# Two transformer layers on one core: every rectified feed-forward bank leaves PSUM through ScalarE's copy

## The reference

```
h = jnp.concatenate([x, -x], axis=-1)
h = s0 * _conn_dense(k0, h)
h = jax.nn.relu(h) * 2          # 512 features: four banks of 128 a sequence ("ff0")
h = s1 * _conn_dense(k1, h)
h = jax.nn.relu(h) * 2          # again four banks a sequence ("ff1")
h = s2 * _conn_dense(k2, h)
```

## Time and profile before

| | |
|---|---|
| median of 3 runs | 815.64 us (815.59 to 815.67) |
| the profiled execution | 815.69 us, its span 813.9 us |
| granted TensorE clock | 0.995 of full speed on the mean |
| TensorE matmul busy | 749.1 us, 92% of the span |
| ScalarE busy | 755.6 us, 93% |
| VectorE busy | 554.7 us, 68% |
| GpSimd busy | 64.1 us, 8% |
| chain that ended last | PE 55%, ACT 25%, DVE 10%, issue 7%, DMA 2% |

### The profile page before, as it was taken

The page is one execution under the profiler, slowest core; times in us unless marked ns, Lnnn a source line. Parts: engine busy times, 40 slices in busy tenths (PEclk is TensorE's granted clock), DMA queues, the critical chain, the costliest instruction groups (busy, mean ns, idle before and its releaser), DMA issues.

```text
span 813.9 us, 18430 instructions
## 1 busy us (share of the span) xinstructions
PE 749.1 (92%) x6975; PEld 250.4 (31%) x6975; DVE 554.7 (68%) x1185; ACT 755.6 (93%) x847; POOL 64.1 (8%) x84
## 2 busy tenths in 40 slices
PE   8888889999999999999999999999998889999997
PEld 5122222342323223232332323232332223333332
DVE  7788786778784687757876677856877476377322
ACT  4899989999999999999999999999989899899986
POOL 4111110000020100201011010101001000000000
PEclk9899999999999999999999999999999999999999
DMA  3916435502256025440265212660353403302500
GB/s 110 196 31 157 97 99 145 128 2 78 79 121 155 14 79 136 107 110 14 92 152 135 53 53 85 144 163 1 106 130 90 120 1 128 82 1 88 133 14 14
DMA packets 46000, 74.12 MB, mean 91 GB/s; under 512 B 7360, under 2 KB 23360, under 8 KB 45776
## 3 DMA queue, kind: packets, MB, share of 16 engines
q1 hardware_dynamic: 44096, 67.31, 32.3%
q0 software_dynamic: 1744, 5.44, 2.2%
q10 hardware_dynamic: 64, 0.10, 0.0%
HBM read 36.84 MB, written 35.65 MB: 89 GB/s over the span
## 4 chain that ended last, share of the span: by engine, by line
PE 55%; ACT 25%; DVE 10%; issue 7%; DMA 2%; SPq 1%; DVEq 0%; ACTq 0%
ACT probs L858 24%; PE ps_pv L1044 23%; PE ps_s L1025 12%; PE ps_misc L883 8%; PE ps_misc L879 6%; PE ps_misc L884 5%; PE ps_misc L872 1%; SPq L576 1%; DMA k_c<-parts_dram 1%; DVE pv_sb L1607 1%; ACT ff_out L810 1%; DVE h_lo L1283 0%; DVE h_hi L1281 0%; DMA k_ab<-thirds_dram 0%; DVE tmp L1145 0%
## 5 line engine op out<-in xcount | busy, mean ns | idle before, releaser
L858 ACT ACTIVATE probs<-ps_s 128x1024 f32<-128x1024 f32 x768 | 723.0, 1062 | 27.8 <-PE ps_s L1025 26.2
L1044 PE MATMUL ps_pv<-probs,v_aug 128*32 128x512 f32 x3072 | 410.2, 606 | 6.3 <-DVE pv_sb L1607 5.6
L1025 PE MATMUL ps_s<-q_ab,k_ab 32*128 32x512 bf16 x896 | 88.4, 384 | 24.4 <-ACT probs L858 21.9
L1025 PE MATMUL ps_s<-q_c,k_c 32*128 32x512 f32 (+1 forms) x640 | 81.8, 500 | 16.6 <-ACT probs L858 16.1
L1044 PEld LDWEIGHTS ps_pv<-probs,v_aug 128*32 128x32 f32 x3072 | 61.2, 108 | 98.0 <-issue 81.6
L883 PE MATMUL ps_misc<-h_hi,k_w 128*128 128x512 f32 x192 | 87.9, 458 | 3.4 <-DVEq L1285 1.2
L884 PE MATMUL ps_misc<-h_lo,k_w 128*128 128x512 f32 x192 | 75.7, 394 | 0.0
L1607 DVE STREAM_TRANSPOSE pv_sb<-ps_pv 128x512 f32<-128x512 f32 x48 | 34.4, 717 | 56.8 <-PE ps_pv L1044 53.0
L883 PEld LDWEIGHTS ps_misc<-h_hi,k_w 128*128 128x128 f32 x192 | 35.8, 187 | 105.5 <-issue 56.2
L1025 PEld LDWEIGHTS ps_s<-q_ab,k_ab 32*128 32x128 bf16 x896 | 22.6, 91 | 144.5 <-ACT probs L858 117.3
L1025 PEld LDWEIGHTS ps_s<-q_c,k_c 32*128 32x128 f32 (+1 forms) x640 | 30.9, 182 | 109.4 <-ACT probs L858 89.5
(11 more groups left out here) (168 smaller groups left out, 619.9 us busy)
## 6 DMA issues: line engine op xcount, KB each, us to landing
parts_dram<-qk_parts SPq DMA_DIRECT2D x38, 256.0 KB, 3.0
parts_dram<-qk_parts SPq DMA_DIRECT2D x16, 512.0 KB, 2.8
q_c<-parts_dram SPq DMA_DIRECT2D x32, 256.0 KB, 5.0
k_c<-parts_dram SPq DMA_DIRECT2D x32, 256.0 KB, 7.1
thirds_dram<-qk_thirds SPq DMA_DIRECT2D x42, 192.0 KB, 2.7
q_ab<-thirds_dram SPq DMA_DIRECT2D x56, 128.0 KB, 3.2
k_ab<-thirds_dram SPq DMA_DIRECT2D x56, 128.0 KB, 3.6
thirds_dram<-qk_thirds SPq DMA_DIRECT2D x28, 128.0 KB, 2.7
```

Source lines behind the costliest of these rows:

```text
L858: nc.scalar.activation(probs[:, U.slot(s), 2 * half:2 * half + 2], ps_s[:, 2 * pair:2 * pair + 2], ACT.Exp, bias=-SCALE[U.layer] * BOUND[U ...
L1025: ins = nc.tensor.matmul(ps_s[:, bank, :], k[row:row + n, slot, c * P:(c + 1) * P], q[row:row + n, slot, :], start=True, stop=True)
L1044: ins = nc.tensor.matmul(ps_pv[32 * j:32 * j + 32, :], v_aug[:, U.v, c, a:a + 32], probs[:, U.slot(s), j, :], start=c == 0 and not odd, st ...
```

## The change

The table `DIRECT` becomes empty. All that asks it (`taker`, `split_ff`, the plan of who frees which bank) then treats the nine banks as the other 55: Relu on ScalarE into `ff_out`, copy and subtraction on VectorE from there.

```
-DIRECT = (("ff0", 1, 0), ("ff0", 2, 0), ("ff0", 3, 0), ("ff0", 4, 0), ("ff0", 5, 0), ("ff0", 6, 1), ("ff1_b", 6, 3), ("ff1_b", 7, 1), ("ff1_b", 7, 3))
+DIRECT = ()
```

## The result

The changed kernel takes 818.36 us (median of 8 runs, 817.5 to 819.59), the kernel before 815.62 (8 runs, 814.66 to 817.06). The ratio is 1.0033, 95% interval 1.0022 to 1.0043: 2.7 us slower, where 3.4 was forecast. The profiled execution took 819.59 us with a span of 817.8, which is 1.2 us above the median, so its total isn't compared; its stretches are. One run of experiment 3 (995.88 us) and one of experiment 8 (2258.81 us) were slow and don't enter the ratios.

A forecast was written before the change was run, and what follows sets the result against it. ScalarE was taken to set the pace in most steps, TensorE in some. Five unit starts at 2.96 us plus unit 20's 0.38 gave 3.34 us on the profiled 815.69, so 819.0 us; range 816.7 to 820.2.

The forecast's parts named there:

- The held `pv`: Starts of units 5, 8, 11, 14, 17: late subtraction delays the transpose and step 2's `pv`, 0.52 or 0.61 us each.
- The forecast chain: Unit starts: from step 0's second exponential through Relu, cast, subtraction and transpose to step 2's `pv`, 2.64 us.
- ScalarE's queue: Unit 8: two Relus and four exponentials delay ScalarE itself by only 0.13 us, inside the 0.61 us shift.
- the sum: 2.96 us at five unit starts plus 0.38 in unit 20, 3.34 us in all; likeliest case, 62%.
- The Relu at 283.77: Start of unit 8 on ScalarE: read as a Relu started from idle, taking 0.60 us.
- the rule that the shifts just add up: All places: TensorE and ScalarE move together in fixed order, so shifts add to 3.34 us; called the weakest point.
- the rival that I gave 8%: Later in each body: another wait ended last anyway and makes up the shift, 815.7 to 816.5 us; 8%.
- Unit 20: The sixth bank, its Relu behind step 1's second exponential: the next exponential ends 0.38 us later.
- The unit ends: Three banks at the ends of units 20 and 22 and in unit 23: ScalarE's idle time covers the Relu, nothing.
- Full price: All nine banks: each Relu costs its full 0.49 us, 4.4 us, 820.1; 13%, including both effects together at 820.5.
- ScalarE's queue alone: Transpose doesn't hold `pv`: five places pay 0.13 us at most, unit 20 0.38; 1.0 us, 816.7; 13%.
- The bank free earlier and not slower: Five unit starts: TensorE's 0.24 us idle before its next job goes, 1.2 us gained, 814.5; 4%.

The follow-up runs named there:

- experiment 3: Kernel before, all nine banks direct, plus a spare Relu of 128x512 on ScalarE at each of the nine places; 817.27 us, ratio 1.0022.
- experiment 8: Kernel before, but VectorE reads the bank once into its own buffer, take next, then cast and subtraction, for sequences 1 to 4 alone; 814.00 us, ratio 0.9981.
- Experiment 2: Changed kernel, but at five unit starts the take goes ahead of bank 0's cast and subtraction, with bank 0's own buffer; 817.09 us, ratio 1.0019.
- experiment 4: Kernel before, plus a VectorE copy of 128x512 after freeing the bank and ahead of the take at five unit starts; 815.97 us, ratio 1.0006.
- experiment 5: Changed kernel with the five unit-start banks direct again, so only the other four go through ScalarE; 816.11 us, ratio 1.0009.
- experiment 7: Kernel before, but at five unit starts VectorE reads the bank once into its own buffer, then take, then cast and subtraction; 814.49 us, ratio 0.9996.
- run 229: Not a follow-up run: "has run 229 instructions" counts ScalarE's instructions ahead of the exponential at step 3 of unit 6; no time or ratio.
- experiment 1: Kernel before, with only the five banks at the starts of units 5, 8, 11, 14 and 17 moved to ScalarE; 817.93 us, ratio 1.0029.
- experiment 6: Changed kernel with the take ahead of bank 0's cast and subtraction at five unit starts, both banks sharing one ff_out; 820.51 us, ratio 1.0070.
- run 230: Not a follow-up run: "has run 230" counts ScalarE's instructions ahead of the same exponential, with one additional instruction; no time or ratio.

## Why the prediction was right

**The held `pv`.** The forecast chain, Relu, cast, subtraction, transpose, `pv`, is there in the predicted order. It takes 2.60 us where 2.64 were summed; the one term that was off is the last, transpose to `pv`, 0.10 for 0.14. Experiment 2 took the hold away with all Relus left on ScalarE, and 0.41 us of 0.56 went; experiment 4 made the take late with no Relu added, and the body grew by as much as the take was late beyond its slack. Both sides of the step are shown.

**ScalarE's queue** was put at 0.13 a body, inside the 0.61. Experiments 2 and 3 show 0.15. Unit 17 is different: the sum held that VectorE has no queue of its own at these places, and there it has one. Experiment 3 pays 0.36 in that unit; in the changed kernel the held `pv` covers it. So the sum was right there without having seen this, which is luck. (The Relu at 283.77, read as one started from idle, in fact started 0.03 before the exponential ahead of it had ended. Its 0.60 us hold all the same: the one at 709.20, after 2.20 us of idle time, takes as long.)

**The size.** By single exponentials the places in units 8, 11, 14 and 17 cost 0.57 each where 0.61 was said, and that in unit 5 0.46 where 0.52 was said. With unit 20's 0.39 that is 3.13 for 3.34. What the sum didn't have is that shifts come and go between the places.

At step 3 of unit 6, 0.25 came back, so the first body cost 0.18. In the kernel before, the first exponential of that step started 0.37 us after the end of its scores, with ScalarE idle for 0.14; in the changed kernel it started 0.10 after them. The traces fall into two groups: 0.37 in the kernel before and in experiments 4, 5, 7 and 8, where ScalarE has run 229 instructions ahead of it, and 0.10 in the changed kernel and in 1, 2, 3 and 6, where it has run 230. In experiment 3 the additional one is a Relu that nobody waits for. So the 0.25 go with the additional instruction in ScalarE's order and not with the held `pv`. What the exponential waited for, the trace doesn't name; it stays open.

At steps 11 and 12 of unit 21 another 0.36 came back, in the changed kernel and in experiments 1, 2, 5 and 6 (0.17 in 4, nothing in 3, 7 and 8). A transpose holds `pv` there as well, for 0.78 us in the kernel before and 0.43 in the changed one, and it starts after VectorE idled 0.46 and 0.10 us. Why is open too. In the changed kernel, and in experiments 2 and 6, some 0.3 were lost again at step 10 of unit 22, which is as unexplained.

In short, 3.13 less 0.25, less 0.36 and plus 0.29 is 2.8, beside the 2.7 measured (interval 1.8 to 3.5). The mechanism and its price at each place were right; the rule that the shifts just add up was right to within 0.3 us. Part of each body's shift made up later is the rival that I gave 8%, and it came at one place of five.

**Unit 20** was put at 0.38 and shows 0.39 at the exponential named. **The unit ends** were put at nothing: shown at two, open at the one in front of a DMA wait.

**The rivals.** Full price: out by experiments 3 and 5. ScalarE's queue alone: that is what experiment 2 is, and the changed kernel isn't. The bank free earlier and not slower: its mechanism is real, TensorE's idle time did go and experiments 7 and 8 show 0.31 a body for it, but in the change it was bought with a later take. The Trainium skill (ScalarE: Activation LUTs, Rules for kernel authors) sends `relu` to VectorE. The measured outcome agrees in sign, but ScalarE's extra work explains only 0.15 of 0.56 us a body.

## What to carry to other kernels

Moving a read of PSUM to the engine that frees the bank sooner is worth only what the next waiter gains, so follow the other engine's queue behind the moved work: here the two instructions that became later stood ahead of a transpose that TensorE needed. Freeing a bank and finishing its processing are two things: one pass into a buffer, the urgent transpose, then the rest gained 0.31 us a body where moving all of it lost 0.56, as long as the queue that takes the third pass has room and the buffer isn't shared with the next bank. Where a total moves by less than its own scatter, the distance between repeated units in one trace, good to 0.04 us here, decides. It takes several bodies that agree: a single one can hold a shift of 0.25 to 0.36 us that nothing in the edit explains, as in units 6, 13 and 21.

## What the runs showed that I had not expected

- A VectorE instruction that nothing waits for is cheaper than its row: the copy of 0.43 us delayed the transpose behind it by 0.27 (experiment 4).
- DMA waits at the start of a late unit vary by 0.6 us between kernels that are the same up to there (1.72 and 2.31 us), as much as a whole body's effect, and behind the longer wait the lower clock cost 0.53 us more.
- In unit 17, a bank's cast that starts 0.43 us late is still 0.44 late ten microseconds on, because VectorE has no gap in which to catch up (experiments 3 and 7).
- A wait's named releaser was wrong just at the place that carries the result: 0.74 us put down to exponentials that had long ended.
